# The bias of the output projection moves from GpSimd into the projection's PSUM bank

## The reference

```python
x = x + 0.5 * ffn(layernorm(x))
x = x + attn(layernorm(x))
x = x + 0.5 * ffn(layernorm(x))
```

```python
y = y.transpose(0, 2, 1, 3).reshape(B, T, C)
return y @ W_proj + b_proj
```

## Time and profile before

| what | value |
|---|---|
| time, median of 3 runs | 488.06 us (486.28 to 489.32) |
| time of the profiled execution | 487.45 us |
| its span, first to last instruction | 485.7 us |
| PE busy | 423.5 us, 87% |
| DVE busy | 406.4 us, 84% |
| ACT busy | 315.0 us, 65% |
| POOL busy | 281.1 us, 58% |
| mean granted TensorE clock | 0.971 |

### The profile page before, as it was taken

The page is one execution under the profiler, slowest core; times in us unless marked ns, Lnnn a source line. Parts: engine busy times, 40 slices in busy tenths (PEclk is TensorE's granted clock), DMA queues, the critical chain, the costliest instruction groups (busy, mean ns, idle before and its releaser), DMA issues. The chain is left out here.

```text
span 485.7 us, 9302 instructions
## 1 busy us (share of the span) xinstructions
PE 423.5 (87%) x2693; PEld 177.7 (37%) x2736; DVE 406.4 (84%) x960; ACT 315.0 (65%) x552; POOL 281.1 (58%) x205
## 2 busy tenths in 40 slices
PE   0779999860799999999999999999999976889996
PEld 0333444430233333333333333333333354424442
DVE  5885555885999999999999999999999988684443
ACT  3423222652999899998998999999989803522221
POOL 5960000234789989899899899898998900000000
PEclk9989999986999999999999999999999997899999
DMA  4300000015753305105013032051002100000001
GB/s 113 88 1 0 1 0 0 1 32 97 230 97 55 67 3 95 27 3 97 22 37 66 16 66 53 0 95 23 0 2 81 37 13 0 2 0 22 0 22 43
DMA packets 18114, 19.50 MB, mean 40 GB/s; under 512 B 4808, under 2 KB 10536, under 8 KB 18088
## 3 DMA queue, kind: packets, MB, share of 16 engines
q1 hardware_dynamic: 17736, 19.11, 18.6%
q10 hardware_dynamic: 352, 0.07, 0.1%
HBM read 13.02 MB, written 6.03 MB: 39 GB/s over the span
## 5 line engine op out<-in xcount | busy, mean ns | idle before, releaser
L1245 POOL TENSOR_TENSOR arena<-arena 128x1024 f32<-128x1024 f32 (+1 forms) x144 | 240.6, 1704 | 29.4 <-ACT arena L1217 28.6
L1178 DVE SCALAR_TENSOR_TENSOR arena<-bank,masks 128x512 f32<-128x512 f32 x288 | 180.1, 691 | 7.7 <-remote 4.2
L1217 ACT ACTIVATE arena<-arena 128x1024 f32<-128x1024 f32 (+1 forms) x160 | 146.1, 958 | 0.8 <-DVE arena L1178 0.2
L1086 PE MATMUL bank<-Q,K 128*128 128x512 bf16 (+3 forms) x352 | 86.7, 326 | 19.1 <-DMA K<-k_parts 11.0
L1207 ACT ACTIVATE bank<-bank 128x128 f32<-128x128 f32 (+7 forms) x128 | 81.3, 635 | 26.2 <-PE bank L1086 26.2
L1184 DVE TENSOR_SCALAR_CACHE_REDUCE bank<-bank 128x128 f32<-128x128 f32 (+7 forms) x128 | 95.5, 780 | 0.0
L1086 PE MATMUL bank<-K,Q 128*128 128x512 bf16 (+3 forms) x381 | 89.8, 328 | 1.7 <-issue 0.6
L1122 PE MATMUL bank<-arena,Vq 128*32 128x512 f32 (+3 forms) x768 | 73.2, 492 | 0.0
L624 ACT ACTIVATE arena<-bank 128x512 f32<-128x512 f32 x40 | 23.9, 597 | 75.3 <-PE bank L499 75.3
L725 DVE TENSOR_TENSOR arena<-arena,bank 128x512 f32<-128x512 f32 x40 | 27.4, 686 | 41.7 <-PE bank L503 41.5
L1086 PEld LDWEIGHTS bank<-Q,K 128*128 128x128 bf16 x384 | 30.2, 98 | 84.2 <-issue 22.2
(11 more groups left out here) (122 smaller groups left out, 352.6 us busy)
## 6 DMA issues: line engine op xcount, KB each, us to landing
Q<-q_parts SPq DMA_DIRECT2D x24, 192.0 KB
K<-k_parts SPq DMA_DIRECT2D x16, 128.0 KB
att<-arena SPq DMA_DIRECT2D x28, 64.0 KB, 1.6
K<-k_parts SPq DMA_DIRECT2D x8, 192.0 KB
X<-in_L_attn_x SPq DMA_DIRECT2D x4, 256.0 KB, 4.6
K<-k_parts SPq DMA_DIRECT2D x16, 64.0 KB
out_x<-X SPq DMA_DIRECT2D x4, 256.0 KB, 2.3
q_parts<-arena SPq DMA_DIRECT2D x3, 256.0 KB
```

The lines of the kernel that those rows point to most:

```text
L1086: last = nc.tensor.matmul(m.bank[:, at + lo:at + hi], left[par][:, g, blk * P:(blk + 1) * P], right[par][:, g, s0:s0 + hi - lo], start=Tru ...
L1178: nc.vector.scalar_tensor_tensor(Y(r, g)[:, y0:y0 + SPAN], m.bank[:, at:at + SPAN], 0.0, mask, ALU.max, ALU.mult).then_inc(relu_done, 1)
L1217: nc.scalar.activation(z, Y(r, g)[:, tile_low(r) - off(r):T - off(r)], ACT.Square)\
L1245: nc.gpsimd.tensor_tensor(z, z, z, ALU.mult).then_inc(fourth_p, 1)
```

## The change

POOL no longer adds `bp` to `X` in `project_qkv`, and so no longer waits there for the normalised tiles. In the merge, PE first writes the bias into each span's bank with four matmuls of the identity by `bp` (128x128 fp32 each), and the four matmuls of the projection then add to what is in the bank. For spans 0, 1 and 3 the bias matmuls stand ahead of PE's wait for that span's `divide`; for span 2 they stand behind a wait for the first two divides, since that bank held denominators which those divides read.

```diff
@@ project_qkv, POOL
-            pool.wait_ge(s.xn_ready, NT - NSPAN)
-            pool.wait_ge(s.xn_ready_a, NSPAN)
-            nc.gpsimd.tensor_tensor(m.X[:, :, :], m.X[:, :, :], m.bp[:, :].unsqueeze(1).to_broadcast([P, NT, C]),
-                                    ALU.add)
             e = (pool.wait_ge, nc.gpsimd.tensor_tensor)
             low_part(e, "q", 0)
             rest_part(e, "q", 1)
@@ Merge.tensor, PE
             for i in range(b * NSPAN // B, (b + 1) * NSPAN // B):
+                if i == 2:
+                    pe.wait_ge(self.att_ready, 2)
+                for k in range(TPS):
+                    nc.tensor.matmul(self.proj_ps[i][:, k * P:(k + 1) * P], m.ident[:, :], m.bp[:, :],
+                                     start=(k == 0), stop=True, skip_group_check=True)
                 pe.wait_ge(self.att_ready, i + 1)
                 for k in range(TPS):
                     t = i * TPS + k
                     last = nc.tensor.matmul(self.proj_ps[i][:, k * P:(k + 1) * P], self.num[:, t * P:(t + 1) * P],
-                                            m.WP[:, :], start=True, stop=True)
+                                            m.WP[:, :], start=False, stop=True, skip_group_check=True)
                 last.then_inc(self.proj_ready, 1)
```

## The result

The changed kernel takes 484.04 us (median of 7 runs, 482.90 to 485.71) against 487.28 us (median of 7, 486.28 to 489.32) for the kernel before in the same session. The ratio is 0.9927 with a 95% interval of 0.9904 to 0.9951: faster by about 0.7%.

A forecast was written before the change was run, and what follows sets the result against it. It took the loads, delayed through DVE's stall behind POOL, to release the attention, and DVE to end last in the merge. Front 2.75 + merge 0.37 = 3.1 us off the median 488.06: 485.0, own range 484.0 to 486.2, full range 483.2 to 487.4.

The forecast's parts named there:

- The front, 2.75 us: Front: without POOL's addition line 921 does not stall, and ACT's next instruction starts 2.75 us earlier; bounds 0 and 3.1.
- The shift is kept through the quads: Quads: everything in the first quad hangs on the loads, so the front's 2.75 us shift is kept.
- The loads take the same 11.07 us: Front: loads issued at 106.16 take the same 11.07 us, land at 117.23, and PE starts at 117.66.
- Batch element 1 stays hidden: Front, DVE: batch element 1's work ends at 113.7, or 116.0 if it loses 2.3 us, before PE starts.
- The bias costs nothing in the merge: Merge: 16 added matmuls, four a span at 1.03 us, fit under DVE's work; cost nothing.
- The faster spread, 0.37 us: Merge: batch element 1's spread takes 1.99 us, not 3.60, so the third divide starts 0.37 us earlier; bounds 0 and 0.37.
- The second pass, nothing: Second feed-forward pass: no gain in the sum, as the standstill ahead of it stays.
- a rival of 1.6 us: More than forecast: next pass's opening PE work runs at full clock, 1.6 us less, 483.4; chance 0.10.
- The rival in which PE becomes late: Merge: at the lower clock throughout, bias groups make PE 4.7 us later, 490.0 in total; chance 0.04.
- The rival in which the front gives nothing: Front: stall has another cause or loads' landing does not follow issue; only 0.37 left, 487.7; chance 0.12.

The follow-up runs named there:

- the last version above: Changed kernel with first batch element's low q on DVE instead of POOL and ACT's line 409 evacuations behind the middle parts: 482.96 us, 0.9910 of before.
- the front alone: Changed kernel without the bias matmuls on PE, so neither POOL nor PE adds the bias: 484.86 us, 0.9940 of before.
- the kernel with one SBUF input: Kernel before with line 921's sum made by a reduction reading one SBUF operand, POOL's addition left in place: 487.08 us, one run.

## Why the prediction was right

It said 485.0 us, faster by 3.1, and 484.04 came, faster by 3.2 by the medians and by 3.6 by the ratio. Its own range, 484.0 to 486.2, held that at its very edge. It held that a difference under 1% can hardly be told from none; seven executions of each did tell 0.7%, with an interval that leaves out 1. The front carries the forecast and is shown; that the sum came so close owes something to luck, as the last two terms show. By its steps:

- **The front, 2.75 us.** It measured 2.77, from line 918 to the first load, and the same in each of the six profiles in which that addition does not stand ahead of POOL's parts and nothing else is moved (11.78 or 11.79). The reason was right too: with POOL's addition and the bias on PE, the 3.27 us are back; with the addition cut up, they end with a piece. That ACT, not DVE, would set the gain (2.75 and not 3.1) holds as well.
- **The shift is kept through the quads.** 266.50 before, 266.34 to 266.52 in all the others.
- **The loads take the same 11.07 us.** They took 10.51. This was no row to add to a sum to 0.1 us: the same loads spread over 0.8 us between executions (10.51 to 11.27), so PE's first matmul, forecast for 117.7, came at 116.84 the first time.
- **Batch element 1 stays hidden.** Line 921 was forecast at 0.16 us both times, and the second took 1.07: it lost 0.9 us under a POOL operation. DVE's last low part still ended at 113.79, 3 us ahead of the loads. The same cover is gone in the last version above.
- **The bias costs nothing in the merge.** Shown by the changed kernel's merge (24.39) against that of the front alone (24.38) and, for the size of the cover, by three times the bias. The cover before the spread was 0.88 and not 0.6 us, since a group behind another takes 0.9 and not 1.03.
- **The faster spread, 0.37 us.** The merge gained 0.49. The step behind it holds less firmly than it was put: the prediction tied the fall of the clock to the standstill of 2.66 us. Without a bias on PE the second spread ran at 3.60, 3.06, 3.61, 1.99, 1.99 and 1.99 us, each behind the same standstill of 2.66 to 2.69 us:

```profile
399.22 1.99 PE L1313 MATMUL bank<-den,spread 128*128 128x256 f32 x8 [2.66 <-DVE den L1367]
```

  This is the kernel with one SBUF input. With the bias it was never slow (seven profiles of seven). So the bias seems to take away a risk that the kernel before had run into in the profile that was read; its 0.49 us are not what every execution of it loses (the merge took 24.38 in three of the five profiles without a bias whose merge is otherwise that of before). Nor is the bias shown to be the cause: of the profiles without it, the two slow ones for which a chip is on record came from one chip, the three at full clock from another, on which no kernel with a single bias is known to have run.
- **The second pass, nothing.** This term was mis-sized: 0.60 us came in the profiles. It was given as a rival of 1.6 us and put aside because the standstill ahead of the pass would stay. The standstill did stay (3.63 us), and still the clock was back sooner. With one bias a span the pass took 73.65 to 73.80 in six profiles; without it 73.75, 74.22, 74.34, 74.35, 75.33 and 75.40. That suggests that PE's work ahead of the pass matters, but does not show it: 74.22, 75.33 and 75.40 come from that other chip, and the kernel with three biases took 74.26 there; on the chip that had both, 73.70 and 73.65 with the bias stand against 73.75 and 74.35 without. What shortened the pass stays open.

The rival in which PE becomes late is the kernel with three biases: its mechanism is real, and its price of some 3 us comes at three times the bias, at full clock. The rival in which the front gives nothing is excluded by the front alone.

## What to carry to other kernels

An operation on an idle engine is not free if it holds something that the engine on the path needs: look in the timeline for a small operation that lasts far longer than its twin and ends when another engine's does, and price the move by the first thing behind it that can't start earlier. Put added work where its engine waits anyway, and measure the end of that cover by doubling or tripling the work. Before a difference between two profiles is put down to an edit, cut both spans at common points and take a second execution: here 0.56 of 4.30 us lay within the loads' own spread.

## What the runs showed of the hardware

- POOL and DVE hold each other, and whichever came first goes through: a DVE addition of one column took 3.27 us instead of 0.16 under a POOL operation, a DVE operation of 128x256 took 4.63 us instead of 0.42, and POOL's addition stretched from 4.54 to 5.47 us behind DVE. A 128x1024 `tensor_scalar` with one operand waits too (3.42 instead of 0.75 us); a 128x1 `tensor_scalar` and a 128x2 reduction under the same POOL operation did not (0.15 and 0.16 us).
- After the same standstill of PE of 2.66 to 2.69 us the spread behind it ran at 3.06 to 3.61 us in three kernels, with the granted clock at 0.51 in the one read for it, and at 1.99 in three others. One standstill in one trace does not tell whether the clock falls.
- From the last store's issue to the first load, with a wait for its landing between them, it took 2.52 or 2.53 us in eleven profiles of thirteen, and 2.82 us in the two with low q on DVE and nothing else moved. The last two stores stood 1.08 us apart in ten profiles (2.52 or 2.53), 0.78 in those two and 0.65 in the last version (2.53), so their distance alone does not explain it.
